# Making ten of 34 weight groups ternary on GpSimd, with the bias additions spread between them, in a graph layer followed by a ternary feed-forward layer

## The reference, cut to what matters

```python
# graph layer: 1250 nodes, 20000 edges, width 512
neigh = segment_sum(xn[src], dst) / max(deg, 1)
h = xn @ W_self + neigh @ W_neigh + b
h = where(h >= 0, h, 0.01 * h)
x = x + h / max(norm(h), 1e-12)
# feed-forward layer, 1408 hidden, weights in groups of 128 along the input
scale = mean(|wg|) + 1e-5
wq = clip(round(wg / scale), -1, 1) * scale      # for w_gate, w_up, w_down
x = x + (silu(x1 @ gate.T) * (x1 @ up.T)) @ down.T
```

## Time and profile before

| | us |
|---|---|
| three runs without the profiler: median (lowest, highest) | 340.61 (340.24, 342.66) |
| the profiled execution's own time | 338.97 |
| its span, first to last instruction | 337.2 |
| mean granted TensorE clock in it | 0.99 |
| PE, DVE, ACT, POOL busy | 317.1, 299.7, 236.9, 169.3 |

### The profile page before, as it was taken

The page is one execution under the profiler, slowest core; times in us unless marked ns, Lnnn a source line. Parts: engine busy times, 40 slices in busy tenths (PEclk is TensorE's granted clock), DMA queues, the critical chain, the costliest instruction groups (busy, mean ns, idle before and its releaser), DMA issues.

```text
span 337.2 us, 5722 instructions
## 1 busy us (share of the span) xinstructions
PE 317.1 (94%) x1521; PEld 239.6 (71%) x1521; DVE 299.7 (89%) x782; ACT 236.9 (70%) x636; POOL 169.3 (50%) x235
## 2 busy tenths in 40 slices
PE   8999999999999998889879999999999999999991
PEld 3444455454555786668659898998989988899981
DVE  3699999999994399998799999999999999999993
ACT  2188988789882357864778786867878688676750
POOL 6025000010102950100015596989889897899992
PEclk9999999999999999999979999999999999999998
DMA  7992322232320021311001111111110100000305
GB/s 211 285 233 68 91 62 65 65 92 83 84 82 25 4 62 54 90 27 24 9 21 25 27 24 29 24 25 28 24 26 16 23 2 1 2 1 1 118 7 182
DMA packets 23610, 19.62 MB, mean 58 GB/s; under 512 B 15230, under 2 KB 16084, under 8 KB 23576
## 3 DMA queue, kind: packets, MB, share of 16 engines
q1 hardware_dynamic: 23498, 19.16, 21.4%
q10 hardware_dynamic: 78, 0.08, 0.1%
HBM read 13.73 MB, written 2.56 MB: 48 GB/s over the span
## 4 chain that ended last, share of the span: by engine, by line
PE 56%; DVE 25%; issue 6%; POOL 5%; DMA 3%; ACT 2%; SPq 1%; DVEq 0%; ACTq 0%; POOLq 0%
PE bank L1409 44%; DVE hot_dst L1098 4%; PE bank L1306 4%; POOL z L719 4%; DVE tq_gu L999 4%; DVE tq_d L999 3%; PE bank L1343 3%; DMA x_sb<-in_x 3%; DVE hot_src L1089 2%; DVE bn L985 1%; DVE bn L1154 1%; DVE x_sb L1151 1%; PE bank L1258 1%; PE bank L1247 1%; DVE z L1133 1%
## 5 line engine op out<-in xcount | busy, mean ns | idle before, releaser
L1409 PE MATMUL bank<-x_hi,t_gu 128*128 128x376 f32 (+1 forms) x264 | 94.8, 359 | 1.5 <-ACT t_gu L875 0.8
L1409 PE MATMUL bank<-x_lo,t_gu 128*128 128x376 f32 (+1 forms) x264 | 93.5, 354 | 0.0
L1306 PE MATMUL bank<-w_sb,xnT 128*125 128x512 f32 x160 | 82.9, 606 | 0.5 <-ACT z L823 0.3
L1206 DVE SCALAR_TENSOR_TENSOR g_acc<-bank,nscale,g_acc 128x376 f32<-128x376 f32 (+1 forms) x99 | 64.0, 646 | 4.6 <-PE bank L1409 3.2
L1206 DVE SCALAR_TENSOR_TENSOR u_acc<-bank,nscale,u_acc 128x376 f32<-128x376 f32 (+1 forms) x99 | 63.8, 645 | 0.2 <-issue 0.2
L732 POOL TENSOR_TENSOR acc<-acc,d_one 128x376 f32<-128x376 f32 (+1 forms) x58 | 63.6, 1101 | 0.0
L679 POOL TENSOR_SCALAR thr<-absum 128x4 f32<-128x4 f32 (+1 forms) x34 | 9.6, 282 | 98.3 <-ACT mag_early L789 74.6
L742 POOL TENSOR_TENSOR hh<-sg,u_acc 128x376 f32<-128x376 f32 (+1 forms) x32 | 35.2, 1100 | 45.2 <-ACT sg L926 45.1
L1409 PEld LDWEIGHTS bank<-x_hi,t_gu 128*128 128x128 f32 x264 | 50.3, 191 | 6.6 <-issue 1.0
L1409 PEld LDWEIGHTS bank<-x_lo,t_gu 128*128 128x128 f32 x264 | 50.3, 190 | 3.4
L1258 PEld LDWEIGHTS bank<-hot_dst,hot_src 128*126 128x126 bf16 x157 | 20.6, 135 | 40.7 <-DVE hot_dst L1098 25.8
(11 more groups left out here) (140 smaller groups left out, 545.6 us busy)
## 6 DMA issues: line engine op xcount, KB each, us to landing
raw<-in_L_ffn_w_gate SPq DMA_DIRECT2D x11, 256.0 KB, 2.7
raw<-in_L_ffn_w_up SPq DMA_DIRECT2D x11, 256.0 KB, 2.6
out_x<-x_sb SPq DMA_DIRECT2D x10, 224.0 KB
raw<-in_L_ffn_w_down SPq DMA_DIRECT2D x8, 256.0 KB, 2.6
turned<-tq_gu SPq DMA_TRANSPOSE x80, 2.4
w_sb<-in_L_gnn_W_neigh SPq DMA_DIRECT2D x1, 1024.0 KB, 6.1
w_sb<-in_L_gnn_W_self SPq DMA_DIRECT2D x1, 1024.0 KB, 7.6
x_sb<-in_x SPq DMA_DIRECT2D x2, 448.0 KB
```

Of the source, the lines that this page charges most:

```text
L1206: nc.vector.scalar_tensor_tensor(out=to, in0=bank_of(u, what)[:, 0:w], scalar=nscale[:, j:j + 1], in1=to, op0=ALU.mult, op1=ALU.add).then_ ...
L1306: last = nc.tensor.matmul(to[0:TP, :], xnT[:, t, k * TP:(k + 1) * TP], w_sb[:, k, half * D:(half + 1) * D], start=k == 0, stop=k == KD - 1)
L1409: last = nc.tensor.matmul(bank_of(u, what)[:, 0:width(u)], w, parts[h], start=h == 0, stop=h == 1)
```

## The change

Ten loads (6, 10, 14, 18, 22 in stage 1; 24, 26, 28, 30, 32 in stage 2) are made ternary by POOL, right after their thresholds, and DVE skips them. POOL has no single operation for it here: it compares each job with its threshold (in place, magnitude becomes 1 or 0), waits for these to be complete, and multiplies the whole load by the weights into the bf16 buffer. They hold 38 jobs, 20 in stage 1 and 18 in stage 2. Two semaphores are added, and whoever waited for `ternary` now waits for both counts. The ten bias additions, which ran ahead of the thresholds of loads 23 to 33, are spread: five before load 23, then one before each pair of loads, four tiles ahead of the neighbour sum that needs it.

```diff
+        POOL_LOADS = (6, 10, 14, 18, 22, 24, 26, 28, 30, 32)
+
+        def wait_ternary(engine, j):
+
+            done = [l for l in range(len(loads)) if load_end[l] <= j]
+            assert load_end[done[-1]] == j
+            mine = sum(loads[l][1] for l in done if l not in POOL_LOADS)
+            pools = sum(l in POOL_LOADS for l in done)
+            engine.wait_ge(ternary, mine)
+            if pools:
+                engine.wait_ge(ternary_pool, pools)
...
-                    sp.wait_ge(ternary, load_end[l - RAWS])
+                    wait_ternary(sp, load_end[l - RAWS])
...
+            def ternary_group(l):
+
+                n = loads[l][1]
+                js = slice(load_end[l] - n, load_end[l])
...
+                mag = (mag_early if l < LOADS1 else mag_late)[:, l % MAGS, 0:n * P]
+                pool.wait_ge(scales, l + 1)
+                for i, j in enumerate(range(js.start, js.stop)):
+                    m = mag[:, i * P:(i + 1) * P]
+                    nc.gpsimd.tensor_scalar(m, m, thr[:, j:j + 1], None, ALU.is_gt).then_inc(mags_over, 1)
+                pool.wait_ge(mags_over, sum(loads[p][1] for p in POOL_LOADS if p <= l))
+                nc.gpsimd.tensor_tensor(to, mag, raw[:, l % RAWS, 0:n * P], ALU.mult).then_inc(ternary_pool, 1)
...
                 scales_of(l)
                 if l < 4:
                     check_windows(l)
+                if l in POOL_LOADS:
+                    ternary_group(l)
             pool.wait_ge(bias_in, 16)
             pool.wait_ge(joined, NB - 1)
-            for t in range(NT):
+
+            def add_bias(t):
+
                 pool.wait_ge(z_out, t + 1)
                 nc.gpsimd.tensor_tensor(z[:, t, :], z[:, t, :], bias_b[0:TP, :], ALU.add).then_inc(z_done, 1)
-            for l in range(LOADS1, len(loads)):
-                scales_of(l)
+
+            for t in range(4):
+                add_bias(t)
+            for n in range(NT):
+                if n + 4 < NT:
+                    add_bias(n + 4)
+                for l in down_loads_in(n):
+                    scales_of(l)
+                    if l in POOL_LOADS:
+                        ternary_group(l)
...
                 if i == 0 and l >= MAGS:
-                    act.wait_ge(ternary, load_end[l - MAGS])
+                    wait_ternary(act, load_end[l - MAGS])
...
             def ternary_of(j):
 
+                if job_load[j][0] in POOL_LOADS:
+                    return
                 dve.wait_ge(scales, job_load[j][0] + 1)
```

More of the change, by code:

```diff
@@ L356, in gnn_ffn, with down_loads_in @@
         NL = len(loads) - LOADS1
+        def down_loads_in(n):
+            lo, hi = (LOADS1 + max(0, min(NL, 2 * i)) for i in (n, n + 1))
+            return range(lo, hi)
         def down_jobs(n):
-            lo, hi = (LOADS1 + max(0, min(NL, 2 * i)) for i in (n, n + 1))
-            return range(load_end[lo - 1], load_end[hi - 1])
+            ls = down_loads_in(n)
+            return range(load_end[ls.start - 1], load_end[ls.stop - 1])
         UNITS = [(0, 0), (0, 1), (1, 0), (1, 1), (0, 2), (1, 2)]
@@ L615, in _ @@
                 if i < TURN_SLOTS:
-                    sp.wait_ge(ternary, load_end[len(loads) - RAWS + i])
+                    wait_ternary(sp, load_end[len(loads) - RAWS + i])
                 else:
@@ L679, in scales_of @@
                 nc.gpsimd.tensor_scalar(thr[:, js], absum[:, js], 0.5 / P, 0.5 * Q_EPS, ALU.mult, ALU.add).then_inc(scales, 1)
+            def ternary_group(l):
+                n = loads[l][1]
+                js = slice(load_end[l] - n, load_end[l])
+                if l < 2 * NF:
+                    to = tq_gu[:, l, :]
+                else:
+                    o, f = down_order[js.start - 2 * NF * KD]
+                    to = tq_d[:, o, f * P:(f + n) * P]
+                mag = (mag_early if l < LOADS1 else mag_late)[:, l % MAGS, 0:n * P]
[5 more added lines that the diff above has]
+                nc.gpsimd.tensor_tensor(to, mag, raw[:, l % RAWS, 0:n * P], ALU.mult).then_inc(ternary_pool, 1)
             def check_windows(part):
@@ L856, in x1_high @@
                 if t == CT[2][0]:
-                    act.wait_ge(ternary, JOBS)
+                    wait_ternary(act, JOBS)
                 c, o, n = place_of(t)
@@ L1080, in _ @@
                     if t - 1 == NT - MAGS:
-                        dve.wait_ge(ternary, JOBS1)
+                        wait_ternary(dve, JOBS1)
                     nc.vector.tensor_tensor(y_lo[:, t - 1, :], bank[4 + (t - 1) % 2][0:TP, :],
@@ L1319, in ternary_in @@
             def ternary_in(f, down):
-                pe.wait_ge(ternary, JOBS if down else JOBS1)
+                wait_ternary(pe, JOBS if down else JOBS1)
                 if not down:
```

2 lines of the change are left out of this document (added).

## The result

The changed kernel took 345.12 us in the median (343.68 to 347.38, four runs), the kernel before 340.43 (339.97 to 342.66): a ratio of 1.0145, 95% interval 1.0101 to 1.0189. By this ratio it is 4.9 us more (3.4 to 6.4). The forecast was 341.6 us, 1.0 us more. The profiled execution took 345.94 us with a span of 344.1.

The account below looks back on a forecast made before the run. DVE was taken to bound stage 1 up to 83 us and tiles 2 to 6 of stage 2, with PE close behind. Stage 1 +0.9 and stage 2 +0.1 made +1.0 us: 341.6 us against the median, range 335 to 348.

Parts of the forecast that it names:

- the likeliest case: Whole kernel: contention roughly cancels the jobs saved, +1.0 us, reaching from 338.5 to 345 us; chance 0.52 including one rival.
- the second rival: Both stages: POOL's comparisons lock DVE out for their whole length, as products do; 348.3 us, chance 0.28.
- Late thresholds and magnitudes: Stage 1: next load's thresholds queue behind POOL's group; 0.1 us each for loads 7, 11 and 15, load 19's 1.3 later.
- signs of being wrong: DVE's mean one-hot matrix duration hardly moves, or DVE waits for thresholds more than 2 us beyond the 2.7 before.
- the cover that I named: Stage 1: DVE takes a load three slots after ACT, so late thresholds cost only 0.1 us for each of three loads.
- Groups 18 and 22 fall into DVE's slack: Stage 1, 83 to 107 us: PE sets the pace, DVE has 4.0 us of slack; +0.3 us for both groups.
- Contention in stage 1: DVE waits out POOL's operations: 0.75 us a product, 0.1 a comparison, 1.15 us a group against 1.05 saved.
- groups 6, 10 and 14: Stage 1 where DVE sets the pace: three times 1.15 less 1.05, plus 0.3 for late thresholds, +0.6 us.
- The start: Stage 2 up to tile 2's neighbour sum: residual step freed of a bias addition, four ternary jobs gone; -1.2 us.
- the late bias addition in tile 6: Stage 2, tile 6: a bias addition now falling there costs 0.3 us.
- The first rival: Both stages: contention is smaller, removed jobs come back in full up to PE's pace; -7.4 us, 333.2 us, chance 0.20.
- The third: Whole kernel: PE is so close behind DVE that saving and loss both vanish; 340.6 us, counted within the forecast's 0.52.

Follow-up runs that it names:

- the 48 comparisons: Kernel before plus four POOL comparisons of 128 columns on each of loads 4 to 15, written to a spare place: +2.8 us (+1.8 to +3.8).
- the part by itself: Bias additions spread and the five groups of stage 2 on POOL, stage 1 as before, against the kernel before: +0.5 us (-0.3 to +1.2).
- the 12 products: Kernel before plus one POOL product of 512 columns on each of loads 4 to 15, written to a spare place: +11.9 us (+10.6 to +13.2).
- four and three groups: Loads 6, 10, 14, 18, or only 6, 10, 14, on POOL, bias additions ahead, against the kernel before: +2.1 and +1.1 us.
- this pair: No POOL groups, bias additions spread, loads 23 to 33 a tile earlier, without and with POOL waiting for DVE, against the kernel before: -0.2 and -1.3 us.

## Why the prediction was right and where it was not

The time lies in the range of 335 to 348, and the direction was as forecast, but the size was not: 4.9 us (3.4 to 6.4) against +1.0. At 345.12 us it is 0.1 us above the 345 at which the likeliest case's own range ends. It is slower by more than 1%, to which the prediction gave 0.30, most of it for the second rival, whose mechanism the 48 comparisons refute. So that the range holds the time is in part luck. The mechanism named, contention eating the saving, fits stage 2. In stage 1, where most of the loss is, it was mostly waits. Step by step:

- **Late thresholds and magnitudes were the term that was mis-sized.** The forecast had 0.1 us more each for loads 7, 11 and 15; they measured 1.4, 0 and 1.0 us more, and load 19 3.0. DVE's waits for thresholds went from 2.7 to 8.1 us, +5.4. Both of the prediction's own signs of being wrong came true: waits more than 2 us beyond the 2.7, and a mean one-hot matrix that hardly moved (271 to 278 ns over the whole span). The groups of stage 1 took 3.9 to 4.9 us from the first comparison on, where the forecast had 3.4 and 0.5 of contention. A comparison of 128 columns takes 0.60 us when free, as long as the one of 157 columns from which I had scaled down to 0.5, and 0.74 us on average in stage 1, since it gives way to DVE. And the cover that I named, three slots between ACT and DVE, wasn't there for load 7: before the change its first ternary job began 0.75 us after its thresholds, and these now came 1.3 us later after load 6's than before, in place of 0.5.
- **"Groups 18 and 22 fall into DVE's slack" failed, and a wait was missed.** These two made most of stage 1's loss: in the profiled executions stage 1 grows by 0.5 us with the first three groups, by 1.8 more with load 18 and by 1.6 more with load 22, where the forecast had 0.3 for both. Load 19's thresholds came 2.1 us later after load 18's than before, in place of 1.3, and DVE stood idle for 3.0 us. The wait of `y_lo` for load 22, 2.4 us, was in the code that the change touches; I had costed only thresholds and magnitudes.
- **Contention in stage 1 was put too high for this kernel, though its prices were near.** Forecast 1.15 us a group; the lengthening grew by 1.4 us for five groups. Alone a product costs 1.0 us and a comparison 0.06, against 0.75 and 0.1 in the sum. In the changed kernel DVE stood idle while four of the five products ran, so they are booked as waits.
- **For groups 6, 10 and 14 the sum came out by luck.** Forecast +0.6 us; the kernel with these alone has +0.5 in the profile of stage 1 and +1.1 (-0.1 to +2.3) in the time. But its terms are 3.2 us more idle time, 0.4 more lengthening and 3.15 of jobs gone, where the forecast had 0.3 of waits and 3.45 of contention.
- The sum of stage 1 with measured terms: idle time of DVE 13.7 us against 6.3, +7.4; lengthening +1.4; jobs gone -5.3: +3.5 us, where the stage grew by 3.7. The forecast had +0.9.
- **Stage 2** came out near its terms but for one. The neighbour sums of tiles 2 and 6 start at 128.28 and 152.48, 6.05 us a tile; forecast 6.1. The start gained 0.8 us and not 1.2. The term that was mis-sized is the late bias addition in tile 6: 0.3 us in the sum, 1.9 measured, for the product of load 32 met the leaky step there and the bias addition the residual. The profile has +1.8 us for the stage, the part by itself +0.5 (-0.3 to +1.2) in the time, the forecast +0.1.
- **The first rival** (little contention) is refuted by the 12 products, **the second** (comparisons lock DVE out) by the 48 comparisons, 2.8 us where it asked for 9 or more. The measured time on that rival's side has another cause: late thresholds and a buffer held, for which it had 1.5 us, not its lock. **The third** (PE hides saving and loss alike) fails too: the time moved by more than its interval. The rule in the Trainium skill, "SBUF — State Buffer", section "Who interferes with whom", holds for products here and for comparisons not at the length it states.

What isn't settled: how much of the 1.0 us in time between four and three groups is real; whether a third magnitude buffer would free the groups, which wasn't tried; and whether the groups of stage 2 cost anything by themselves.

## What to carry to other kernels

Work moved to an idle engine has to be costed by how long it holds its buffers and what stands behind it in that engine's queue, not by the busy time saved: here DVE saved 0.26 us a job and POOL held each load of four jobs for about 4 us, with the next thresholds behind it. List every wait that names the moved work, and the last user of the buffer, before calling it covered. On DVE and POOL, put two-input POOL operations where DVE reads PSUM, takes statistics or waits: the neighbour sum at 140.42 us took 0.74 us and the statistics at 120.39 us before the change 0.69 beside a bias addition, as elsewhere. The same ten bias additions cost 5.5 us of lengthening in one order and 1.6 in another. What lengthening costs in time depends on who waits next: all of it in stage 1 with the added operations, 1.1 of 3.9 us in this pair.

## What the runs showed of the hardware

A one-input comparison of 128 columns on POOL takes 0.60 us free and costs DVE 0.06 us; beside a busy DVE it takes 0.78 us itself. The one multiply-add of 132 columns on record took 0.31, so at about this shape the comparison takes twice as long. A two-input product of 512 columns takes 1.27 us, beside DVE too, and costs DVE 1.0. When both have a queue of two-input operations they take turns one by one: among four bias additions, which took 1.29 to 1.35 us each, four of seven jobs of DVE took 1.37 to 1.42 us in place of 0.34. The engine with the short operations loses most.
